# Moving the last step of two layer norms from VectorE to GpSimd in an early-fusion transformer block

## The reference

```python
h = concat([layernorm(patches(x) @ W + b, cls) * gamma + beta, txt])   # 37 + 128 = 165 tokens of 256
q, k, v = split(layernorm(h) @ W_qkv.T + b_qkv)                        # 16 heads of 16
s = q @ k.T / 16
s = where(s among the 49 largest of its row, s, -inf)                  # int(165 * 0.3)
h = h + softmax(s) @ v @ W_out.T + b_out
x2 = layernorm(h)
h = h + moe(x2) + (silu(x2 @ Wg) * (x2 @ Wu)) @ Wd                     # 64 experts, top 8, capacity 128
```

## Time and profile before

| | |
|---|---|
| runs | 3135.48, 3138.24 and 3142.18 us; median 3138.24 us |
| profiled execution, first to last instruction | 3227.4 us |
| share of the span busy | PE 82%, DVE 79%, ACT 77%, POOL 68% |
| granted TensorE clock, mean | 0.925 of full speed |

### The profile page before, as it was taken

The page is one execution under the profiler, slowest core; times in us unless marked ns, Lnnn a source line. Parts: engine busy times, 40 slices in busy tenths (PEclk is TensorE's granted clock), DMA queues, the critical chain, the costliest instruction groups (busy, mean ns, idle before and its releaser), DMA issues. The chain is left out here.

```text
span 3227.4 us, 81090 instructions
## 1 busy us (share of the span) xinstructions
PE 2638.8 (82%) x21777; PEld 2097.4 (65%) x21777; DVE 2551.2 (79%) x11421; ACT 2482.0 (77%) x11137; POOL 2207.5 (68%) x4328
## 2 busy tenths in 40 slices
PE   4688988988888888888888988888888888637774
PEld 3566766766666676666666766666766666437664
DVE  1798999989899899889899898988999888613221
ACT  2998988988888888889888898888989889301110
POOL 3467777777777777777777777777777777544554
PEclk8799999999999999999999999999999999858897
DMA  2001000001010000110000000101011000037774
GB/s 60 11 24 23 19 23 20 20 24 24 18 24 20 23 22 17 24 24 20 22 20 23 22 19 20 24 20 24 18 24 24 19 18 17 7 78 187 178 187 84
DMA packets 184206, 118.99 MB, mean 37 GB/s; under 512 B 100304, under 2 KB 175244, under 8 KB 183724
## 3 DMA queue, kind: packets, MB, share of 16 engines
q1 hardware_dynamic: 149356, 94.33, 10.6%
q0 software_dynamic: 34368, 19.34, 4.0%
HBM read 66.81 MB, written 33.40 MB: 31 GB/s over the span
## 5 line engine op out<-in xcount | busy, mean ns | idle before, releaser
L843 ACT ACTIVATE JK<-S,thr 128x165 f32<-128x165 f32 x2688 | 1120.5, 422 | 23.2 <-POOL thr L607 16.6
L664 POOL DMA_INDIRECT slot_token<-TOKI,SLOT x512 | 545.7, 1066 | 225.0 <-issue 193.7
L645 POOL TENSOR_SCALAR X<-S,nt 128x165 f32<-128x165 f32 x1344 | 590.4, 456 | 76.0 <-DVE LIST L1106 67.0
L831 ACT ACTIVATE E<-bank,nb 128x165 f32<-128x165 f32 x1344 | 517.0, 407 | 96.4 <-POOL cnt L627 78.6
L843 ACT ACTIVATION_READ_ACCUMULATOR JK<-S,thr 128x1 f32 x2688 | 512.3, 191 | 0.0
L1223 DVE SCALAR_TENSOR_TENSOR PR<-S,TV,E 128x165 f32<-128x165 f32 x1344 | 457.1, 395 | 0.0
L1031 DVE TENSOR_SCALAR_CACHE_REDUCE S<-bank 128x165 f32<-128x165 f32 x1344 | 361.5, 318 | 67.4 <-PE bank L1573 34.7
L1106 DVE MAX8 LIST<-X 128x8 f32<-128x165 f32 x1344 | 351.1, 316 | 5.4
L1589 PE MATMUL bank<-IDENT,PR 128*128 128x128 f32 x1344 | 224.3, 284 | 126.9 <-DVEq L1214 69.5
L1096 DVE TENSOR_TENSOR X<-X,flip 128x495 int32<-128x495 int32 x448 | 297.6, 665 | 0.0
L1593 PE MATMUL bank<-IDENT,PR 128*37 128x128 f32 x1408 | 293.3, 291 | 0.0
(11 more groups left out here) (201 smaller groups left out, 6633.1 us busy)
## 6 DMA issues: line engine op xcount, KB each, us to landing
S<-in_w_gate SPq DMA_DIRECT2D x64, 192.0 KB
S<-in_w_up SPq DMA_DIRECT2D x64, 192.0 KB
E<-in_w_down SPq DMA_DIRECT2D x64, 192.0 KB
x_rows<-X SPq DMA_DIRECT2D x64, 160.0 KB
H<-in_txt SPq DMA_DIRECT2D x64, 128.0 KB
QA<-QT SPq DMA_DIRECT2D x512, 10.3 KB
QB<-QT SPq DMA_DIRECT2D x512, 10.3 KB
out<-OT SPq DMA_DIRECT2D x64, 128.0 KB
```

What stands on the lines that cost most here:

```text
L645: last = pool.tensor_scalar(X[n % DEEP][:, t % GROUP, :], S[r % 2][:, t, :], nt[r % 2][:, t:t + 1], DOWN, ALU.add, ALU.mult)
L664: pool.indirect_dma_start(slot_token, bass.IndirectOffsetOnAxis(SLOT[r % 2][:, 0, k:k + 1], 0), TOKI[r % 2][:, :], None, bounds_check=SLOT ...
L831: act.activation(E[r % 2][:, t, :], chunks(bS[g % 3], GROUP, T)[:, t % GROUP, :], ACT.Exp, bias=nb[:, t:t + 1], scale=-1.0, accum_out=sz[: ...
L843: act.activation(JK[:, t % 4, :], S[r % 2][:, t, :], ACT.Sign, bias=(t0, t1)[n][:, t:t + 1], scale=-1.0, accum_out=(c0, c1)[n][:, t:t + 1] ...
```

## The change

The last step of both norms, subtracting the mean and multiplying by the inverse deviation, moves from DVE to POOL. POOL gets a third small instruction for each norm, which negates the mean (`nm`, `bnm`), and then computes (h + negated mean) times scale. X2 is made on POOL behind the second half of the refinement of nt, at the end of the iteration, ahead of the X tiles of the next one; XN is made behind `rs`, between X groups 1 and 2. There are own semaphores for the two results, s_xn and s_x2, which PE, SP and POOL wait for; the counts of s_fd and s_bd shrink by two. DVE's aggregations now wait until POOL is through with the batch before.

```diff
-        s_fd, FD = sem("s_fd"), 5
+        s_fd, FD = sem("s_fd"), 3
-        s_fg, FG = sem("s_fg"), 6
+        s_fg, FG = sem("s_fg"), 7
-        s_bd, BD = sem("s_bd"), 27
+        s_bd, BD = sem("s_bd"), 25
-        s_bg, BG = sem("s_bg"), 2
+        s_bg, BG = sem("s_bg"), 3
+        s_xn, s_x2 = sem("s_xn"), sem("s_x2")
...
             def store_x(b, r):
-                sp.wait_ge(s_bd, BD * b + 19)
+                sp.wait_ge(s_bd, BD * b + 17)
+                sp.wait_ge(s_x2, 2 * b + 2)
...
                 pool.tensor_tensor(rs[:, :], ve[:, :], PW[:, :], ALU.pow).then_inc(s_fg, 1)
+                pool.tensor_scalar(nm[:, :], mv[:, :, 0], -1.0, None, ALU.mult).then_inc(s_fg, 1)
+
+            def front_norm2(b, r):
+                pool.wait_ge(s_fg, FG * b + 3)
+                ahead(pool, s_fp, FP * (b - 1) + 1, b - 1 if known(b) else b)
+                gated()
+                pool.tensor_scalar(XN[:, 0, :], H[r][:, 0, :], nm[:, 0:1], rs[:, 0:1], ALU.add, ALU.mult).then_inc(s_xn, 1)
+                pool.tensor_scalar(XN[0:IMG, 1, :], H[r][0:IMG, 1, :], nm[0:IMG, 1:2], rs[0:IMG, 1:2],
+                                   ALU.add, ALU.mult).then_inc(s_xn, 1)
 
             def front_bias(b, r):
 
-                pool.wait_ge(s_fd, FD * b + 5)
+                pool.wait_ge(s_xn, 2 * b + 2)
...
                 pool.tensor_tensor(brs[:, :], bve[:, :], PW[:, :], ALU.pow).then_inc(s_bg, 1)
+                pool.tensor_scalar(bnm[:, :], bmv[:, :, 0], -1.0, None, ALU.mult).then_inc(s_bg, 1)
+
+            def back_norm(b, r):
+                pool.wait_ge(s_bg, BG * b + 3)
+
+                ahead(pool, s_xrow[r % 2], of_ring(b - 2, r % 2, 2, 32), b - 2 if known(b) else b)
+                gated()
+                for c in range(2):
+                    pool.tensor_scalar(X2[r % 2][:, c, 0:D], HM[:, c, :], bnm[:, c:c + 1], brs[:, c:c + 1],
+                                       ALU.add, ALU.mult).then_inc(s_x2, 1)
...
                 if has(i + 1):
                     front_scale2(i + 1)
+                    front_norm2(i + 1, (r + 1) % RING)
...
                 if has(i):
                     refine2(i, r, 1)
+                if has(i - 2):
+                    back_norm(i - 2, (r - 2) % RING)
...
             def front_norm_aggr(b):
                 dve.wait_ge(s_fd, FD * b + 2)
+                ahead(dve, s_fg, FG * b, b - 1 if known(b) else b)
...
             def back_aggr(b):
                 dve.wait_ge(s_bd, BD * b + 5)
+                ahead(dve, s_bg, BG * b, b - 1)
...
-                if has(i - 3):
-                    back_norm(i - 3, (r - 3) % RING)
...
-                if has(i + 1):
-                    front_norm2(i + 1, (r + 1) % RING)
...
             def front_xt(b):
-                pe.wait_ge(s_fd, FD * b + 5)
+                pe.wait_ge(s_xn, 2 * b + 2)
...
             def back_xt(b, r):
-                pe.wait_ge(s_bd, BD * b + 9)
+                pe.wait_ge(s_x2, 2 * b + 2)
```

More of the change, by code:

```diff
@@ L124, in early_fusion_kernel @@
         rs = sb("rs", [P, 2])
+        nm = sb("nm", [P, 2])
         XN = sb("XN", [P, 2, D])
@@ L177, in early_fusion_kernel @@
         brs = sb("brs", [P, 2])
+        bnm = sb("bnm", [P, 2])
         X2 = [sb(f"X2{n}", [P, 2, XW]) for n in range(2)]
@@ L409, in store_out @@
             def store_out(b, r):
-                sp.wait_ge(s_bd, BD * b + 12)
+                sp.wait_ge(s_bd, BD * b + 10)
                 gated()
@@ L1011, in front_norm_aggr @@
                 dve.bn_aggr(mv[0:IMG, 1, :], st[0:IMG, 1, :]).then_inc(s_fd, 1)
-            def front_norm2(b, r):
-                dve.wait_ge(s_fg, FG * b + 2)
-                ahead(dve, s_fp, FP * (b - 1) + 1, b - 1 if known(b) else b)
-                dve.tensor_scalar(XN[:, 0, :], H[r][:, 0, :], mv[:, 0, 0:1], rs[:, 0:1], ALU.subtract, ALU.mult).then_inc(s_fd, 1)
-                dve.tensor_scalar(XN[0:IMG, 1, :], H[r][0:IMG, 1, :], mv[0:IMG, 1, 0:1], rs[0:IMG, 1:2],
-                                  ALU.subtract, ALU.mult).then_inc(s_fd, 1)
             def take(i, r, g):
@@ L1248, in back_aggr @@
                 dve.bn_aggr(bmv[:, 1, :], bst[:, 1, :]).then_inc(s_bd, 1)
-            def back_norm(b, r):
-                dve.wait_ge(s_bg, BG * b + 2)
-                ahead(dve, s_xrow[r % 2], of_ring(b - 2, r % 2, 2, 32), b - 2 if known(b) else b)
-                for c in range(2):
-                    dve.tensor_scalar(X2[r % 2][:, c, 0:D], HM[:, c, :], bmv[:, c, 0:1], brs[:, c:c + 1],
-                                      ALU.subtract, ALU.mult).then_inc(s_bd, 1)
             def back_glu(b):
@@ L1281, in back_top2 @@
             def back_top2(b):
-                dve.wait_ge(s_bd, BD * b + 14)
+                dve.wait_ge(s_bd, BD * b + 12)
                 gated()
@@ L1646, in back_down @@
             def back_down(b):
-                pe.wait_ge(s_bd, BD * b + 11)
+                pe.wait_ge(s_bd, BD * b + 9)
                 for c in range(2):
```

24 lines of the change are left out of this document (12 added, 12 removed).

## The result

| | median, us | range, us | runs |
|---|---|---|---|
| before | 3136.86 | 3131.65 to 3142.18 | 4 |
| after | 3312.07 | 3305.20 to 3317.07 | 4 |

The ratio is 1.0566 [1.0543, 1.0589]. The change costs 175 us where 63 were forecast: the direction is right, the time lies outside the range (3158 to 3265).

What follows compares the result with a forecast made beforehand. A loop of waits through PE and DVE, 42.6 us a batch, was taken as the bound. PE's 0.78 and DVE's 0.55 us, the later counting, became 1.0 us over 63 batches: 3138 + 63 = 3201 us, range 3158 to 3265.

Steps and rivals of the forecast that it cites:

- The prices on POOL: Each of the four X2 and XN instructions takes 0.55 us on POOL, each of the two negations 0.2 us.
- high-end rival: Memory port slows POOL's four new instructions to about 0.73 us each, giving 3233 us; chance 0.08.
- PE's path: X2 from POOL is 1.05 us late; without slack up to L1551, PE loses 0.78 us a batch in the mean.
- The X tiles and RD: Later X tiles on POOL start DVE 1.8 us later; RD's idle time absorbs 1.25, leaving 0.55 us a batch.
- XN costs nothing: XN is ready on POOL before PE asks for it, with 1 to 2 us of cover, so PE loses nothing.
- The sum: The later of PE's 0.78 and DVE's 0.55 us counts in each batch, taken as 1.0 us: 63 us; chance 0.66.
- DVE's relief: If DVE's own work closes the batches, 1.40 us a batch is gained, giving 3050 us; chance 0.07.
- absorption: A PE stall before ACT's VZ, ending at its own time, swallows the delays: no change, 3140 us; chance 0.07.
- POOL the bound: POOL's delay reaches the thresholds ACT counts for and returns through nt: 2.0 us a batch, 3264 us; chance 0.12.
- PE's wait over 60 us: Sign in the changed profile: PE's wait ahead of the X2 transposes rises from 30.7 us to 60 or more.
- 43.83 us from X2 to X2: Sign: 43.6 us from one X2 to the next; 42.6 us or less would make the prediction wrong.
- A wait at the count of over 1 us a batch: Sign: DVE newly waits 1 us or more a batch for POOL's X at the count, before next to none.

Runs made afterwards that it cites:

- X2 alone: The kernel after with XN put back on DVE in its old place, only X2 on POOL: 3268.7 us, ratio 1.0428.
- XN alone: The kernel after with X2 put back on DVE in its old place, only XN on POOL: 3232.46 us, ratio 1.0319.
- POOL's load alone: The kernel before plus six POOL instructions of the same sizes and places on scratch tiles nobody reads: 3254.28 us, ratio 1.0381.
- the one kernel that held it up behind X2: The kernel after with six products of constants on PE ahead of its wait for X2: 3446.8 us, ratio 1.0536 to before.

## Why the prediction was wrong

- **The prices on POOL**: right. 548 ns for X2 and XN against 0.55, 0.24 for a negation against 0.2. The high-end rival (the port slows these four) is refuted: they range from 541 to 553 ns in the groups. The six new instructions take 170 us in all, as forecast (166); POOL's busy time is up by 135 us only (2217.6 to 2352.8 on the quick chips), because other rows of it are shorter, the X tiles for one (585.7 to 574.4).
- **PE's path: a step that failed.** X2 comes 1.41 us late, where 1.05 was forecast and 0.78 left in the mean. "Between the X2 transposes and L1551 PE has no slack" was read as a constant of 20.14 us from two batches, both at full clock. In the same profile the mean of 52 batches is 21.21 us, and on the quick chips it goes from 20.89 to 22.37. So L1551 comes 1.41 + 1.48 = 2.89 us later where 0.78 was priced. With X2 alone the difference is the granted clock: PE idles longer ahead of X2, 41 batches are low instead of 17, and a low batch needs 2.0 us more. In after it is the clock and POOL's tiles side by side.
- **The X tiles and RD: the other step that failed.** "RD's idle time takes 1.25 of this in the mean" subtracted a slack that the timed chips don't have (7.2 us in all, 0.11 a batch). From the start of DVE's count to L1551 it is 13.77 us in before and 13.81 with X2 alone, whose count starts 2.43 us late: all of that delay goes through. Group 3 of the tiles came 2.70 us later (2.6 forecast). Without the subtraction DVE is 1.8 us late: 63 x 1.8 = 113, 3251 us, inside the range but still 61 us short of what was measured.
- **XN costs nothing**: right for PE, wrong for the whole. XN alone costs 1.0319, by the tiles and by `off`.
- **Put at nothing without a reason**: DVE's small tensor_scalar instructions, held by POOL's additions, 0.68 us a batch in after. The additions last as long as before; moved, they meet other instructions. I had weighed the port only for the four new instructions and not for those which shift along with POOL's queue.
- **The sum**: 2.16 to the count plus 0.71 behind it, 2.87 us, against 1.0. The form was right, the later of two paths counts; both were priced too low. POOL's load alone costs 117 us and X2 alone 131, after 175.
- **The rivals**: DVE's relief (0.07) and absorption (0.07) are refuted; DVE's busy time fell by 38 us (2555.5 to 2517.7 on the quick chips) and not by 85, as 43 of its relief are spent inside `off`. POOL the bound (3264 us) was nearest in size, and partly so in mechanism: POOL's order is one of two paths, but not by ACT's thresholds.
- **What would show it**: PE's wait over 60 us (148.4) came, but before has 61.8 itself on the quick chips, so the mark of 60 us told nothing. 43.83 us from X2 to X2 came as well (43.6 forecast), but it was set against 42.6 from what looks like a slower chip; on the quick one it is (2755.7 - 170.8) / 63 = 41.0 before. A wait at the count of over 1 us a batch didn't (23.6 us in all), because DVE comes there just as late. RD's idle time didn't get smaller (10.4 us after 7.2).

Open: whether holding the clock up in after on a quick chip would win anything. The estimate above says 0.2 us a batch; the one kernel that held it up behind X2 ran on a slower chip, brought X2 1.04 us later than in after, and after was not run beside it.

## What to carry to other kernels

Before a slack is subtracted, set the span of the profiled execution against the timed runs: a profile 2.8% longer than they are may have its waits in other places. A stretch that is read as fixed wants more than two batches. Price a late input of TensorE with what follows it at both granted clocks: with X2 alone on POOL the idle time was paid a second time in the clock (1.56 us and 0.92 us a batch up to DVE's count). Then ask what stands right behind, for in after most of that second payment was hidden beside POOL's tiles. And when an engine is given more work, everything behind it in its queue moves: look what DVE does beside each of those instructions, not beside the new ones alone.

## What the runs showed of the hardware

- Five chips ran the kernel before in 3135 to 3140 us (three) and 3236 and 3268 us (two). In the profile of before, which looks like the slower kind, PE pauses inside its row of short matmuls of the context, where the profile shows nothing that it waits for (38.7 us in all; 27.2 to 42.7 us in the six profiles from the slower chips, no such wait in before or after on the quick ones):

```profile
492.95 0.70 PE L1615 MATMUL bank<-PTT,VZ 128*32 128x165 f32 x4
494.05 0.44 PE L1615 MATMUL bank<-PTT,VZ 128*32 128x165 f32 x2 [0.39 <-issue]
```

- A DVE tensor_scalar on 6 or 9 columns takes 0.17 us in the median, and up to 1.77 us when POOL's additions (0.72 us each) run beside it. Moving them some 18 us further along took 61.6 us out of these and put 16 us into other DVE instructions.
- A POOL tensor_scalar on 128x256 with two per-partition operands takes 548 ns, 37 partitions of it 542.
